# Three stages of weight maxima, and constant products in TensorE's waits, in a two-layer graph attention kernel

## The reference

```
h = jnp.maximum(_layernorm(x, axis=-1), 0.0)
x = x + _L0_gnn_ref(h, L0_gnn_Wq, L0_gnn_bq, ..., adj)
h = jnp.maximum(_layernorm(x, axis=-1), 0.0)
x = x + _L1_gnn_ref(h, L1_gnn_Wq, L1_gnn_bq, ..., adj)

# one layer
q = _heads(seq_inputs @ Wq + bq); k = _heads(seq_inputs @ Wk + bk); v = _heads(seq_inputs @ Wv + bv)
scores = jnp.einsum('bhqd,bhkd->bhqk', q, k) / np.sqrt(HEAD_SIZE)
bias = jnp.where(graph_mask, 0.0, NEG)[:, None]
probs = jax.nn.softmax(scores + bias, axis=-1)
ctx = jnp.einsum('bhqk,bhkd->bhqd', probs, v)
return ctx @ Wf + bf
```

## Time and profile before

| what | value |
|---|---|
| median of three runs | 1850.08 us |
| the profiled execution's own time | 1853.11 us |
| its span, first to last instruction | 1851.3 us |
| mean granted TensorE clock | 0.995 of full speed |
| PE busy | 1821.8 us, 98% |
| DVE, ACT, POOL busy | 1621.9, 1561.2, 1490.9 us |

### The profile page before, as it was taken

How to read it: one execution, slowest core, us unless ns; L and a number is a source line. 1 busy time by engine, 2 the same in 40 slices (tenths; PEclk the granted TensorE clock), 3 DMA queues, 4 the chain that set the end, 5 groups by cost and what they waited for, 6 DMA issues and landing times.

```text
span 1851.3 us, 54324 instructions
## 1 busy us (share of the span) xinstructions
PE 1821.8 (98%) x17210; PEld 1050.4 (57%) x17210; DVE 1621.9 (88%) x5551; ACT 1561.2 (84%) x4793; POOL 1490.9 (81%) x1781
## 2 busy tenths in 40 slices
PE   7899999999999999999999999999999999999998
PEld 3455555555555555555555555555555555555555
DVE  7889898898988988889888888988889888898876
ACT  5888888888888888888888888888888888888884
POOL 4678888888888888888888888888888888888761
PEclk8999999999999999999999999999999999999999
DMA  6656666666666666666667666667666666666655
GB/s 195 175 171 185 204 205 193 197 205 199 208 197 199 200 193 209 205 197 194 193 207 203 203 196 200 201 199 215 195 196 194 198 207 197 200 179 193 194 169 180
DMA packets 439942, 363.32 MB, mean 196 GB/s; under 512 B 207700, under 2 KB 406888, under 8 KB 439656
## 3 DMA queue, kind: packets, MB, share of 16 engines
q1 hardware_dynamic: 439656, 359.86, 65.1%
HBM read 184.30 MB, written 175.37 MB: 194 GB/s over the span
## 4 chain that ended last, share of the span: by engine, by line
PE 86%; DVE 4%; DMA 3%; SPq 3%; issue 2%; ACT 1%; POOL 1%; DVEq 0%; ACTq 0%; POOLq 0%
PE ps_qk L683 12%; PE ps_shared L683 12%; PE ps_shared L685 12%; PE ps_shared L684 12%; PE ps_qk L684 12%; PE ps_qk L685 12%; PE ps_shared L780 7%; PE ps_scores L800 7%; SPq L375 2%; DMA p_dram<-p_blocks 1%; DVE probs L1316 1%; DMA p_moved<-p_dram 1%; DVE qk_lo L1296 1%; POOL probs L551 1%; ACT probs L1013 1%
## 5 line engine op out<-in xcount | busy, mean ns | idle before, releaser
L1013 ACT ACTIVATE probs<-probs,row_min 128x128 f32<-128x128 f32 x1512 | 583.1, 391 | 2.5 <-DVE row_rcp L1281 1.5
L551 POOL TENSOR_TENSOR probs<-probs,row_rcp 128x768 f32<-128x768 f32 x252 | 370.2, 1469 | 215.5 <-DVE row_rcp L1281 215.2
L1316 DVE CUSTOM_DVE_ANT_0 probs<-ps_scores,mask,minus_scale 128x128 f32<-128x128 f32 x1512 | 429.6, 347 | 0.9 <-issue 0.6
L568 POOL TENSOR_TENSOR p_half<-p_moved,p_half 128x768 f16<-128x768 f32 x236 | 388.0, 1644 | 1.6 <-ACT p_half L988 1.6
L1296 DVE SCALAR_TENSOR_TENSOR qk_lo<-ps_qk,qk_bias,qk_hi 128x512 f16<-128x512 f32 x384 | 278.7, 747 | 77.2 <-ACT qk_hi L996 76.1
L1013 ACT ACTIVATION_READ_ACCUMULATOR probs<-probs,row_min 128x1 f32 x1512 | 288.8, 191 | 0.0
L996 ACT ACTIVATE qk_hi<-ps_qk,qk_bias 128x512 f16<-128x512 f32 x384 | 258.1, 672 | 14.6 <-PE ps_qk L685 14.6
L547 POOL TENSOR_TENSOR x_tile<-x_tile,out_bias 128x384 f32<-128x384 f32 x256 | 257.7, 1007 | 1.1 <-DVE out_bias L1240 1.1
L1327 DVE SCALAR_TENSOR_TENSOR x_tile<-ps_shared,out_scale,x_tile 128x384 f32<-128x384 f32 x256 | 157.1, 613 | 111.2 <-PE ps_shared L685 108.6
L683 PE MATMUL ps_shared<-wf_hi,ct_hi 128*128 128x384 f16 x768 | 250.6, 326 | 2.4 <-DVE ct_lo L1290 2.4
L685 PE MATMUL ps_shared<-wf_hi,ct_lo 128*128 128x384 f16 x768 | 250.8, 327 | 0.0
(11 more groups left out here) (152 smaller groups left out, 3997.7 us busy)
## 6 DMA issues: line engine op xcount, KB each, us to landing
p_dram<-p_blocks SPq DMA_DIRECT2D x256, 384.0 KB, 2.4
p_moved<-p_dram SPq DMA_DIRECT2D x1008, 96.0 KB, 2.4
h_dram<-h_blocks SPq DMA_DIRECT2D x252, 192.0 KB, 2.6
h_moved<-h_dram SPq DMA_DIRECT2D x1008, 48.0 KB, 2.0
x_tile<-in_x SPq DMA_DIRECT2D x128, 192.0 KB, 2.9
out_x<-x_tile SPq DMA_DIRECT2D x128, 192.0 KB, 2.7
adj_u<-in_adj SPq DMA_DIRECT2D x64, 64.0 KB, 2.6
p_half<-p_dram SPq DMA_DIRECT2D x16, 96.0 KB, 2.3
```

Of the source, the lines that this page charges most:

```text
L551: nc.gpsimd.tensor_tensor(probs_of(t, i), probs_of(t, i), row_rcp[i % 2][:, :].rearrange("p (a o) -> p a o", o=1) .to_broadcast([P, HEADS, ...
L568: nc.gpsimd.tensor_tensor(p_part(i, 1), p_moved[i % 2][:, :, :].rearrange("p a n -> p (a n)"), p_part(i, 0), ALU.subtract).then_inc(p_set, 1)
L1013: ins = nc.scalar.activation(tile[:, s, :], tile[:, s, :], ACT.Exp, bias=row_min[i % 2][:, s:s + 1], scale=-1.0, accum_out=row_sum[i % 2][ ...
L1316: ins = nc.vector.tensor_tensor_reduce(tile[:, s, :], score_bank(i, s // PAIRS)[:, (s % PAIRS) * P:(s % PAIRS + 1) * P], mask[b][:, i, :], ...
```

## The change

The maxima of layer 0 go round in two stages in place of one, so that with layer 1's there are three. Stage 0 takes queries and keys (with the maxima of their biases), stage 1 the outputs; stage 2 is layer 1's as before. `largest` is set to zero first, since its other columns are transposed before they are written. `find_scales` is cut into `bound_in`, `bound_out`, `top_power`, `set_in_scales` and `set_out_scale`. On PE stage 0 stands ahead of the first `project_v`, and stage 1 with `sum_out_bias(0)` stands among the first query and key pieces. The orders of ACT and DVE in the beginning are written anew around that. SP's order is untouched, and POOL gets one more memset at its start.

`keep_busy` can now write another bank, and 26 more constant products are issued: 13 in the beginning, six ahead of `score(1,0)`, seven between two `output` of the last but one unit.

```diff
@@ PE
-            def turn_largest(l):
-                pe.wait_ge(largest_found, 5 * (l + 1))
+            def turn_largest(stage):
+                l = stage // 2
+                pe.wait_ge(largest_found, (4, 5, 10)[stage])
...
             def score(t, i):
                 b = unit_no(t) % 2
+                wait(pe, masked, unit_count(t, PER, i - 1))
+                if (t, i) == (1, 0):
+
+                    keep_busy(6, score_bank(i, 0))
...
                 output(A, 0)
+                keep_busy(7, ps_qk[1])
                 output(A, 1)
...
             share_value_peak()
+            keep_busy(4)
             turn_first(1)
             keep_busy(2)
             turn_first(2)
+            keep_busy(2)
             turn_first(3)
             turn_largest(0)
+            keep_busy(4)
+            share_largest(0)
+            keep_busy(3)
             project_v(0, 0)
             project_v(0, 1)
-            share_largest(0)
             project_v(0, 2)
             project_v(0, 3)
+            for piece in range(6):
+                project_qk(0, piece)
+            turn_largest(1)
+            for piece in range(6, 9):
+                project_qk(0, piece)
+            share_largest(1)
             sum_out_bias(0)
-            for piece in range(12):
+            for piece in range(9, 12):
                 project_qk(0, piece)
             project_v(1, 0)
@@ ACT
             h_hi(0, 3)
+            weights_hi(0, 0)
+            v_out(0, 0)
             relu(1, 0)
+            v_out(0, 1)
+            weights_hi(0, 1)
             relu(1, 1)
-            v_out(0, 0)
-            v_out(0, 1)
+            v_out(0, 2)
             relu(1, 2)
-            weights_hi(0, 0)
...
@@ DVE
+            find_peaks(0)
             weights_lo(2)
...
+            take_largest(0)
+            bound_in(slice(0, 2))
+            top_power(slice(0, 2))
+            set_in_scales(0, slice(0, 2))
+            first_lo(2)
+            statistics(1, 0)
+            first_lo(3)
+            weights_lo(0)
+            find_score_scales(0)
+            h_turn(1, 0)
...
```

More of the change, by code:

```diff
@@ L664, in share_value_peak, with share_largest @@
                           ).then_inc(value_shared, 1)
-            def share_largest(l):
-                pe.wait_ge(peaks_set, l + 1)
-                pe.matmul(small_bank(l)[:, H:H + 6], ones[0:6, :], peaks[:, :], start=True, stop=True).then_inc(largest_shared, 1)
+            def share_largest(stage):
+                pe.wait_ge(peaks_set, stage + 1)
+                pe.matmul(small_bank(stage // 2)[:, H:H + 6], ones[0:6, :], peaks[:, :], start=True, stop=True).then_inc(largest_shared, 1)
             def sum_out_bias(l):
@@ L685, in three, with keep_busy @@
                 return pe.matmul(acc, a_lo, b_hi, start=False, stop=last)
-            def keep_busy(products):
+            def keep_busy(products, free=ps_shared[0]):
                 for _ in range(products):
-                    pe.matmul(ps_shared[0][:, :], idle_work[:, 0:P], idle_work[:, :], start=True, stop=True)
+                    pe.matmul(free[:, :], idle_work[:, 0:P], idle_work[:, :], start=True, stop=True)
             def turn_first(i):
@@ L918, in _ @@
             project_qk(1, 7)
-            turn_largest(1)
+            turn_largest(2)
             project_qk(1, 8)
-            share_largest(1)
+            share_largest(2)
             for piece in range(9, 12):
@@ L1098, in _ @@
             h_hi(0, 3)
+            weights_hi(0, 0)
+            v_out(0, 0)
             relu(1, 0)
+            v_out(0, 1)
+            weights_hi(0, 1)
             relu(1, 1)
-            v_out(0, 0)
-            v_out(0, 1)
+            v_out(0, 2)
             relu(1, 2)
-            weights_hi(0, 0)
-            weights_hi(0, 1)
-            weights_hi(0, 3)
-            v_out(0, 2)
-            make_mask(0)
-            h_hi(1, 0)
-            relu(1, 3)
-            for chunk in range(3):
-                qk_hi_out(0, chunk)
+            v_out(0, 3)
+            h_hi(1, 0)
+            qk_hi_out(0, 0)
+            make_mask(0)
+            relu(1, 3)
+            qk_hi_out(0, 1)
+            h_hi(1, 1)
+            qk_hi_out(0, 2)
+            weights_hi(0, 3)
             relu(2, 0)
             qk_hi_out(0, 3)
-            h_hi(1, 1)
             relu(2, 1)
-            v_out(0, 3)
             h_hi(1, 2)
@@ L1194, in first_lo, with find_peaks @@
                                         ht_hi[0][:, :, rows], ALU.subtract).then_inc(first_set, 1)
-            def find_peaks(l):
-                dve.wait_ge(largest_turned, l + 1)
-                then(nc.vector.tensor_reduce(peak[:, :], small_bank(l)[0:6, H:H + P], AX_X, ALU.max))
+            def find_peaks(stage):
+                dve.wait_ge(largest_turned, stage + 1)
+                then(nc.vector.tensor_reduce(peak[:, :], small_bank(stage // 2)[0:6, H:H + P], AX_X, ALU.max))
                 nc.vector.tensor_scalar(peaks[:, :], ident[0:6, 0:6], peak[:, :], None, ALU.mult).then_inc(peaks_set, 1)
-            def take_largest(l):
-                dve.wait_ge(largest_shared, l + 1)
-                nc.vector.tensor_copy(largest_all[:, :], small_bank(l)[:, H:H + 6]).then_inc(largest_taken, 1)
@@ L1439, in _ @@
             first_lo(1)
+            find_peaks(0)
             weights_lo(2)
-            find_largest_bias(0)
-            find_largest(0, 3)
-            statistics(1, 0)
-            first_lo(2)
-            first_lo(3)
-            statistics(1, 1)
-            find_peaks(0)
-            statistics(1, 2)
-            h_turn(1, 0)
-            take_largest(0)
-            find_scales(0)
-            h_turn(1, 1)
-            find_other_scales(0)
-            spread_v_bias(0)
-            weights_lo(0)
+            take_largest(0)
[8 more added lines that the diff above has]
+            h_turn(1, 0)
+            statistics(1, 1)
+            spread_v_bias(0)
+            weights_lo(1)
+            h_turn(1, 1)
+            statistics(1, 2)
+            find_largest(0, 3)
+            qk_lo_out(0, 0)
             h_turn(1, 2)
             statistics(1, 3)
+            find_peaks(1)
+            qk_lo_out(0, 1)
+            take_largest(1)
+            bound_out()
+            top_power(slice(3, 4))
+            set_out_scale(0)
+            h_turn(1, 3)
             statistics(2, 0)
-            weights_lo(1)
+            keep_out_bias(0)
             statistics(2, 1)
-            qk_lo_out(0, 0)
-            h_turn(1, 3)
-            keep_out_bias(0)
-            qk_lo_out(0, 1)
             weights_lo(3)
@@ L1487, in _ @@
             invert_sums(0, 0)
-            find_peaks(1)
-            take_largest(1)
+            find_peaks(2)
+            take_largest(2)
             probs_turn(0, 0)
-            find_scales(1)
+            bound_in(slice(0, 3))
+            bound_out()
+            top_power(slice(0, 4))
+            set_in_scales(1, slice(0, 3))
+            set_out_scale(1)
             invert_sums(0, 1)
```

46 lines of the change are left out of this document (29 added, 17 removed).

## The result

The changed kernel takes 1861.9 us (median of six runs, 1860.6 to 1863.6) against 1849.9 of the kernel before in the same comparison: a ratio of 1.0065, 95% interval [1.0054, 1.0076]. It is slower, as forecast, but by 12.0 us where 5.7 were forecast, and the time lies outside the range of 1846.0 to 1859.5. The profiled execution's span is 1861.8 us, 10.5 more than before.

What follows compares the result with a forecast made beforehand. PE was taken as the bound (busy 1821.8 of 1851.3 us), changeable only where it waits or clocks low. 8.0 - 1.0 - 1.3 = +5.7 gave 1858.8 profiled, 1855.8 us as median; range 1846.0 to 1859.5.

Steps and rivals of the forecast that it cites:

- Stage 0 works: Beginning: take_largest(0) near 16.0 instead of 21.77, wq_hi ending at 18.6, 5.8 us earlier than before.
- PE's wait for chunk 0: Beginning: PE, done near 27, waits some 4 us for the bank of chunk 0 until its evictions.
- the chain `h_lo(1,0)`, `bring_h(1,2)`, value weights, scores: Beginning: gate to the first scores through unit 1's layer norm, 12.1 us from 31.95 to 44.06, carried over unchanged.
- term three: Last units: seven constant products fill PE's 2.35 us wait and keep the clock up; -1.3 us, between -1.7 and -0.5.
- Term two: Ahead of score(1,0): six constant products in PE's 2.37 us wait keep the clock up; -1.0 us, between -1.7 and +0.4.
- The rival by which the clock drops all the same: Shorter remaining waits still lower the clock, so both clock gains are nothing: +8.0, 1858.1 us; chance 0.10.
- Term one: Beginning: h_lo(1,0) ends at 40.0 instead of 31.9, first scores at 52.1; +8.0 us, from +4 to +9.
- the sign: Beginning: wq_hi ending before 19 us would show that stage 0 goes as worked out.
- From `statistics` to `relu`: Beginning, layer norm: from the end of statistics over POOL to the start of relu, 1.44 us taken from a row.
- 0.7 off for overlapping hand-offs: Beginning: next DVE or ACT instruction starts some 0.08 before the last one's shown end; 0.7 us over nine steps.
- costs nothing, but it would cost up to 3.0: Beginning: sum_out_bias(0), moved behind piece 8, lies beside DVE's and ACT's wait for relu(1,3); up to 3.0 us without it.

Runs made afterwards that it cites:

- no_products: The changed kernel without any of the 26 new constant products; median 1863.8 us, ratio 1.0067 to the kernel before.
- warm_scores: The changed kernel with 14 more constant products ahead of score(0,0); median 1857.9 us, ratio 1.0037 to the kernel before.
- both_warm: The changed kernel with evictions earlier on ACT, statistics earlier on DVE, and 14 products ahead of score(0,0); 1851.6 us, ratio 1.0006 to the kernel before.
- bias_first: The changed kernel with sum_out_bias(0) back ahead of stage 1 and keep_out_bias(0) ahead of the second eviction; 1861.9 us, ratio 1.0064 to the kernel before.
- all_orders: both_warm with SP's order changed too: load_out_bias(1) behind the weight, adjacency and x loads, bring_h(1,2) and keep_h(1,3); 1850.6 us, ratio 0.9998 to the kernel before.
- all_bias: all_orders with sum_out_bias(0) back ahead of stage 1 and keep_out_bias(0) ahead of the second eviction; 1849.6 us, ratio 1.0001 to the kernel before.
- evict_first: The changed kernel with ACT's first two evictions moved ahead of relu(1,2) and relu(1,3); median 1857.5 us, ratio 1.0039 to the kernel before.

## Why the prediction was wrong in size

**Right.** Stage 0 works and nothing comes of it; PE's wait for chunk 0 (3.99, forecast some 4); the chain `h_lo(1,0)`, `bring_h(1,2)`, value weights, scores (12.4 us, carried as 12.1); term three (-1.2 to -1.4, forecast -1.3). Term two is right by the spans (-0.7, forecast -1.0), but in part by luck: its reason, that the clock falls there without the products, holds in the kernel before and did not in the changed one (`no_products`, clock 1.00 behind 2.46 us). The rival by which the clock drops all the same did not come about: behind waits of 1.07 and 0.84 us the clock stays at 1.00. By the rule weighed for it (the Trainium skill, TensorE: Matmul & The Clock Gate, A second HAM failure mode: psum-queue depth-cycling) it would have dropped, and the traces here do not bear that out.

**Term one is the step that failed: +8.0 forecast, +12.1 at the first scores and +15.2 at score(1,0), where the range allowed +9.** It had two prices at nothing: what DVE's splits do to POOL beside them, and what the clock costs behind the longer wait. What it missed is made up of:
- First weights, **1.4**. `take_largest(0)` came at 17.42 and not at 16.0, and `wq_hi` ended at 19.87 where I had named 19 as the sign. In this execution layer 0's value weights landed late (their maximum starts at 6.48; 5.10 to 5.67 in all the others), and in the kernels made from the changed one the same instruction ran at 15.2 to 16.5, around the forecast's 16.0. This part belongs to the one execution.
- POOL beside DVE, **1.8** by `h_turn(1,1)` (end 28.4, forecast 25.2, less the 1.4). From `statistics` to `relu` I took 1.44 from a row in which DVE had no split beside it. The change puts each split right behind a `statistics`, so POOL's tiny instructions are held by it twice, for 2.4 together, 0.6 of it under other waits. The Trainium skill (SBUF — State Buffer, Who interferes with whom) says that a DVE instruction with two SBUF inputs contends with a GpSimd instruction that reads SBUF. The rows agree: `wq_lo` is made of `p_half` and `wq_hi`. The traces show that the two go together; that the shared read is the cause, no run here tests. The trace of before had one such case that I passed over:

```profile
28.75 1.03 POOL L538 TENSOR_SCALAR shift<-mean_var,rstd 128x1 f32<-128x1 f32 x1
```

  0.26 alone, and DVE's split began at 28.26.
- **0.5** in the steps behind that, where I had taken 0.7 off for overlapping hand-offs, and 0.4 in the carried 12.1. With the two above this makes the 4.1 between 52.1 and 56.20.
- The clock, **3.1**, between `score(0,0)` and `score(1,0)`. I used the clock to cost the products, and costed it at nothing for the waits that my own delay makes. The wait ahead of the first scores grew from 1.09 to 3.84 us, longer than both waits behind which I had seen the clock fall. Shown by `warm_scores` and `both_warm`, where the 14 products bring the stretch back to 25.0.

**A cost put at nothing that is not nothing.** Of `sum_out_bias(0)` I said that it "costs nothing, but it would cost up to 3.0" without the wait. In the changed kernel it is indeed hidden (`bias_first`: 0.0). Once `h_lo(1,0)` is on time it shows, by 1.2 at the last eviction and 0.9 at the scores (`all_orders` against `all_bias`), and not over PE's 3.0 but over POOL's additions. The medians do not show it: each against before in its own group, they stand at +0.1 and +0.6. I had named what stands behind it on PE, not who waits for its result. The scores of `all_bias` are still 1.8 later than before. Of that, 1.3 is the 14 products themselves, which outlast the wait that they were put into, and 0.5 is the last eviction (44.52 against 44.01). Fewer products, or `statistics(2,1)` earlier, weren't tried.

**What is left open.** The 10.5 us of the spans are 12.1 + 3.1 - 0.7 - 1.3 (the steady part) - 1.4 (term three) - 1.3 (the end, from the third last `add_residual` on, which the forecast did not have and no run explains); how the medians' 12.0 divide can't be told that finely, since the steady part alone, where all do the same work, differs by up to 4.7 us between executions. How much of `evict_first`'s 5.8 at the scores is its order, and how much its earlier first weights (1.3 at `take_largest(0)`), the runs don't separate.
